# A two-part vision kernel on one core: the next image's moments moved, the picks in fewer instructions, and motif rows left out at the edges

## What is computed

```python
# feature: (2, 128, 128, 96); G = 16 groups of Cg = 8 planes, K = 3
slices = [feature[:, :, ki:ki + Hm, kj:kj + Wm] for ki in range(K) for kj in range(K)]  # Hm = 126, Wm = 94
motif = stack(slices).reshape(B, G, 9, Cg, L)
gram = einsum('bgjcl,bgjdl->bgjcd', motif, motif)
d2 = sq[..., :, None] + sq[..., None, :] - 2.0 * gram        # the diagonal set to inf
nn_idx = argmin(d2, axis=-1)
u_max = max(nn_idx, axis=-1)
c_max = sum(nn_idx == u_max[..., None], axis=-1)
motif_nn = take_along_axis(motif, u_max[..., None, None], axis=3)
term = floor(motif * motif_nn * c_max[..., None, None] / Cg)
ser2 = (motif * batch_mask + term).reshape(B, G, Cg, 9, Hm, Wm)
for k in range(9):                                            # ki, kj = k // 3, k % 3
    out[:, :, :, ki:ki + Hm, kj:kj + Wm] += ser2[:, :, :, k]
x = x + out
```

## Time and profile before

| | us |
|---|---|
| median of 3 runs | 1446.81 (1444.57 to 1449.93) |
| the profiled execution | 1437.17 |
| its span | 1435.4 |
| TensorE busy | 1302.0 (91%) |
| VectorE busy | 1123.1 (78%) |
| ScalarE busy | 887.5 (62%) |
| GpSimd busy | 635.8 (44%) |

### The profile page before, as it was taken

One profiled execution on the slowest core, in us unless ns is written; L12 is line 12 of the kernel. 1 busy time (PEld: TensorE's weight loads), 2 busy tenths in 40 slices (PEclk: granted clock), 3 DMA queues, 4 the chain that ended last, 5 costly groups with the idle time before them and its releaser, 6 DMA issues. The chain is left out here.

```text
span 1435.4 us, 34146 instructions
## 1 busy us (share of the span) xinstructions
PE 1302.0 (91%) x13586; PEld 1051.4 (73%) x13586; DVE 1123.1 (78%) x1896; ACT 887.5 (62%) x1013; POOL 635.8 (44%) x672
## 2 busy tenths in 40 slices
PE   3899999986999499999979999999779959999998
PEld 1799997985999255555549999989679945555554
DVE  6587775568763799999967777737877739999998
ACT  3567663212552499999956666531145419999996
POOL 4889992442220253343039999624323114444400
PEclk9999999998999699999999999999989969999999
DMA  5466731892134345464427886239105234264433
GB/s 218 129 210 214 218 96 32 255 262 118 46 132 180 132 138 126 127 166 101 133 86 225 255 250 189 75 107 275 35 2 243 112 136 142 78 179 119 139 74 106
DMA packets 77173, 210.28 MB, mean 146 GB/s; under 512 B 15450, under 2 KB 15558, under 8 KB 74326
## 3 DMA queue, kind: packets, MB, share of 16 engines
q1 hardware_dynamic: 62510, 158.10, 35.0%
q0 software_dynamic: 6720, 36.93, 9.7%
q10 hardware_dynamic: 7784, 13.07, 3.3%
HBM read 91.54 MB, written 67.04 MB: 110 GB/s over the span
## 5 line engine op out<-in xcount | busy, mean ns | idle before, releaser
L1780 PE MATMUL acc<-rnd,ident 128*128 128x376 f32 x1152 | 392.8, 484 | 13.6 <-ACT rnd L1757 13.6
L1780 PEld LDWEIGHTS acc<-rnd,ident 128*128 128x128 f32 x1152 | 216.8, 192 | 134.5 <-ACT rnd L1757 15.0
L954 PE MATMUL ps_a<-wa,shared 128*128 128x192 f16 x1536 | 295.0, 246 | 2.6 <-DMA xc<-low 1.5
L954 PE MATMUL ps_a<-wb,xb 128*128 128x192 f16 x1536 | 294.0, 245 | 0.0
L1752 ACT ACTIVATE rnd_m<-prod,plus_round,scale 128x1504 f32<-128x1504 f32 x144 | 235.6, 1636 | 38.8 <-DVE prod L1603 29.5
L1716 DVE SCALAR_TENSOR_TENSOR over<-prod,scale,rnd 128x1504 bf16<-128x1504 f32 x144 | 255.0, 1773 | 0.0
L572 POOL TENSOR_TENSOR vt<-z 96x256 f32<-96x256 f32 x248 | 241.6, 995 | 3.8 <-ACT z L848 3.6
L1757 ACT ACTIVATE rnd<-rnd_m,minus_round 128x1504 f32<-128x1504 f32 x144 | 223.2, 1550 | 4.7
L1660 POOL DMA_INDIRECT near<-f_planes,index x42 | 120.4, 2867 | 148.0 <-DVE prod L1603 141.9
L954 PE MATMUL ps_a<-wfa,shared 128*128 128x96 f16 x1536 | 155.7, 206 | 5.9 <-issue 5.6
L954 PE MATMUL ps_a<-wfb,xb 128*128 128x96 f16 x1536 | 155.8, 205 | 0.9 <-issue 0.9
(11 more groups left out here) (344 smaller groups left out, 2463.9 us busy)
## 6 DMA issues: line engine op xcount, KB each, us to landing
xb<-shared ACTq DMA_DIRECT2D x64, 195.0 KB, 2.8
f_planes<-img SPq DMA_DIRECT2D x8, 1536.0 KB, 14.2
shared<-f_planes SPq DMA_DIRECT2D x16, 768.0 KB, 5.5
v_a<-shared SPq DMA_DIRECT2D x40, 260.0 KB, 2.6
v_b<-xb SPq DMA_DIRECT2D x40, 260.0 KB, 3.0
shared<-v_a SPq DMA_DIRECT2D x40, 260.0 KB, 4.4
xb<-v_b SPq DMA_DIRECT2D x40, 260.0 KB, 5.1
v_c<-xc SPq DMA_DIRECT2D x40, 195.0 KB, 3.5
```

The costliest lines, as they stand in the source:

```text
L954: mm = lambda a, w, first, end: nc.tensor.matmul(out(i), a, w, start=first, stop=end)
L1780: nc.tensor.matmul(o(m), k["ident"][:, :], rnd[:, n % RNDS, BR * m:BR * m + BR, :], start=False, stop=False, skip_group_check=True)
```

## The change

There are three edits.

1. The moments of image 1 are computed in `motif_grams` of image 0 instead of in `motif_terms`. Their small tiles lie in `x_next`, whose contents are used up by then, and their sums in the PSUM bank `ps_s`.
2. The picks leave out a copy of the PSUM tile `nnt` (it is read from PSUM twice instead), and two of the small operations are merged into others. Two results that the next instruction does not read are no longer waited for.
3. A step of `motif_terms` works on the rows that `valid(n)` names: at slab 0 one row less for ki = 1 and two less for ki = 2, at slab 7 two less for ki = 0 and one less for ki = 1. The memsets of the edge rows and the semaphore `edged` go.

```diff
@@ ScalarE in motif_grams, ahead of its copies into g_half
+            if x_after is not None:
+                group_stats_root(nc, act, k, next_sums, next_mom, att_sems["stat_summed"], att_sems["stat_rooted"])
             for j in (0, 2):
                 act.wait_ge(chunk_done, C // CHUNK + j // 2)
@@ TensorE in motif_grams, behind last_column()
+            def next_summed(step, line):
+                pe.wait_ge(att_sems["stat_ready"], step + 1)
+                nc.tensor.matmul(next_sums[:, step, :], k["mean_ones"][:, :], next_part[:, line, :], start=True,
+                                 stop=True).then_inc(att_sems["stat_summed"], 1)
+
+            def next_columns():
+                pe.wait_ge(att_sems["mom_row"], 1)
+                for j in range(2):
+                    last = nc.tensor.matmul(next_col[0:C, j:j + 1], next_mom_c[0:1, j, :], k["ident"][0:1, 0:1],
+                                            start=True, stop=True)
+                last.then_inc(att_sems["mom_col"], 1)
+
             for side in range(2):
                 for m_ in range(m, BLOCKS):
+                    if x_after is not None and side == 0 and m_ == m:
+                        next_summed(0, 3)
                     gram(m_, range(8 * side, 8 * side + 8))
+                if x_after is not None:
+                    if side == 0:
+                        next_summed(1, 1)
+                    else:
+                        next_columns()
@@ VectorE in motif_grams, ahead of its copies into g_half
+            if x_after is not None:
+                channel_moments(nc, dve, c, k, next_part, next_mom, next_mom_c, next_sums, next_col, att_sems)
             for j in (1, 3):
                 dve.wait_ge(chunk_done, C // CHUNK + j // 2)
@@ the picks, VectorE
-            c.then_wait(nc.vector.tensor_copy(nnt, ps_a[1][0:MG, 0:MR]))
+            nnt = ps_a[1][0:MG, 0:MR]
-            c.then_wait(nc.vector.tensor_tensor(t1, u, jj_less, ALU.subtract))
-            c.then_wait(nc.vector.tensor_scalar(ge, t1, 0.0, None, ALU.is_ge))
-            c.then_wait(nc.vector.tensor_scalar(t1, t1, float(KK), None, ALU.add))
+            nc.vector.scalar_tensor_tensor(t1, u, float(KK), jj_less, ALU.add, ALU.subtract)
+            c.then_wait(nc.vector.tensor_tensor(ge, u, jj_less, ALU.is_ge))
             c.then_wait(nc.vector.scalar_tensor_tensor(ku, ge, -float(KK), t1, ALU.mult, ALU.add))
-            c.then_wait(nc.vector.scalar_tensor_tensor(cu, ge, -1.0, jj, ALU.add, ALU.add))
-            c.then_wait(nc.vector.tensor_scalar(t1, ku, 3.0, None, ALU.is_ge))
-            c.then_wait(nc.vector.tensor_scalar(t2, ku, 6.0, None, ALU.is_ge))
-            c.then_wait(nc.vector.tensor_tensor(kui, t1, t2, ALU.add))
+            nc.vector.scalar_tensor_tensor(cu, ge, -1.0, jj, ALU.add, ALU.add)
+            c.then_wait(nc.vector.tensor_scalar(t2, ku, 3.0, None, ALU.is_ge))
+            c.then_wait(nc.vector.scalar_tensor_tensor(kui, ku, 6.0, t2, ALU.is_ge, ALU.add))
@@ motif_terms
+        def valid(n):
+            i, sh = steps[n]
+            dy = TAPS[sh][0]
+            return max(dy - R * i, 0), min(R, HM + dy - R * i)
...
-            fv = fc[:, s, :].rearrange("p (r c) -> p r c", c=C)[:, :, dx:dx + WM]
+            lo, hi = valid(n)
+            fv = fc[:, s, :].rearrange("p (r c) -> p r c", c=C)[:, lo:hi, dx:dx + WM]
...
-            nc.gpsimd.memset(near[:, 0, 0:2 * C], 0.0).then_inc(edged, 1)
...
-            if b + 1 < B:
-                channel_moments(nc, dve, c, k, part, mom, mom_c, next_sums, next_col, att_sems)
...
-                nc.vector.scalar_tensor_tensor(over[:, n % 2], prod[:, n % PRODS], scale[:, sh:sh + 1],
-                                               rnd[:, n % RNDS], ALU.mult, ALU.is_lt).then_inc(over_done, 1)
+                rows = slice(*valid(n))
+                nc.vector.scalar_tensor_tensor(over[:, n % 2, rows], prod[:, n % PRODS, rows], scale[:, sh:sh + 1],
+                                               rnd[:, n % RNDS, rows], ALU.mult, ALU.is_lt).then_inc(over_done, 1)
```

More of the change, by code:

```diff
@@ L1123, in motif_grams @@
         mn = sb("mn", [MR, MG], F32)
-        nnt, eq2 = (g_half[0:MG, j, 0:MR] for j in range(2))
+        eq2 = g_half[0:MG, 1, 0:MR]
         sel = g_half[0:MG, 2, 0:6 * KK].rearrange("p (v j) -> p v j", j=KK)
@@ L1140, in motif_grams @@
         sums = lambda: ps_s[:, 0:2 * GN].rearrange("p (a g) -> p a g", g=GN)
+        if x_after is not None:
+            x_flat = x_next[:].rearrange("p a c -> p (a c)")
+            next_part = x_flat[:, 0:4 * GN].rearrange("p (a g) -> p a g", g=GN)
+            next_mom = x_flat[:, 4 * GN:6 * GN].rearrange("p (a g) -> p a g", g=GN)
+            next_mom_c = x_flat[0:1, 6 * GN:6 * GN + 2 * C].rearrange("p (a c) -> p a c", c=C)
+            next_sums, next_col = sums(), ps_s[:, 2 * GN:2 * GN + 2]
         piece = lambda j: img[:, :, PIECE * j:PIECE * j + PIECE]
@@ L1559, in motif_terms @@
         acc = [ctx.enter_context(nc.psum_tensor(f"acc{s}_{b}", [P, R // BR, 512], F32)) for s in range(2)]
[L1560 to L1563, removed]
+        (own, scaled, indexed, prod_v, prod_p, rm_done, rnd_done, over_done, acc_done, out_ready, last_rows) = (
+            sem(n) for n in ("t_dve", "scaled", "indexed", "prod_v", "prod_p", "rm_done",
                              "rnd_done", "over_done", "acc_done", "out_ready", "last_rows"))
@@ L1751, in _ @@
                     act.wait_ge(rnd_done, n - 1)
-                nc.scalar.activation(rnd_m[:, n % 2], prod[:, n % PRODS], ACT.Identity,
+                rows = slice(*valid(n))
+                nc.scalar.activation(rnd_m[:, n % 2, rows], prod[:, n % PRODS, rows], ACT.Identity,
                                      bias=k["plus_round"][:, 0:1], scale=scale[:, sh:sh + 1]).then_inc(rm_done, 1)
@@ L1756, in _ @@
                     act.wait_ge(acc_done, n - RNDS + 1)
-                nc.scalar.activation(rnd[:, n % RNDS], rnd_m[:, n % 2], ACT.Identity,
+                nc.scalar.activation(rnd[:, n % RNDS, rows], rnd_m[:, n % 2, rows], ACT.Identity,
                                      bias=k["minus_round"][:, 0:1]).then_inc(rnd_done, 1)
@@ L1767, in _ @@
                 if sh == 0:
-                    if i == 0 and b + 1 < B:
-                        channel_moments_sums(nc, pe, k, part, mom_c, next_sums, next_col, att_sems)
-                    if i == 1 and b + 1 < B:
-                        pe.wait_ge(att_sems["mom_col"], 2)
                     if i >= 2:
@@ L1776, in _ @@
                                          start=True, stop=False, skip_group_check=True)
-                o = lambda m: bank[:, m, 0:BR * C].rearrange("p (r c) -> p r c", c=C)[:, :, dx:dx + WM]
+                lo, hi = valid(n)
+                spans = [(m, max(lo - BR * m, 0), min(hi - BR * m, BR)) for m in range(R // BR)]
+                o = lambda m, a, e: bank[:, m, 0:BR * C].rearrange("p (r c) -> p r c", c=C)[:, a:e, dx:dx + WM]
                 pe.wait_ge(rnd_done, n + 1)
-                for m in range(R // BR):
-                    nc.tensor.matmul(o(m), k["ident"][:, :], rnd[:, n % RNDS, BR * m:BR * m + BR, :], start=False,
+                for m, a, e in spans:
+                    nc.tensor.matmul(o(m, a, e), k["ident"][:, :], rnd[:, n % RNDS, BR * m + a:BR * m + e, :], start=False,
                                      stop=False, skip_group_check=True)
                 pe.wait_ge(over_done, n + 1)
-                for m in range(R // BR):
-                    last = nc.tensor.matmul(o(m), k["minus_ident"][:, :], over[:, n % 2, BR * m:BR * m + BR, :],
+                for m, a, e in spans:
+                    last = nc.tensor.matmul(o(m, a, e), k["minus_ident"][:, :], over[:, n % 2, BR * m + a:BR * m + e, :],
                                             start=False, stop=(sh == KK - 1), skip_group_check=True)
```

13 lines of the change are left out of this document (2 added, 11 removed).

## The result

The changed kernel took 1433.79 us (median of 13 runs, 1428.63 to 1440.93) against 1444.89 us for the kernel before (13 runs, 1435.75 to 1450.81) in the same comparison: 0.9936 of its time, interval 0.9915 to 0.9957, some 9 us less. The first three of the latter 13 runs are those behind the median of 1446.81. The forecast of 1441.4 us was too high and the range of 1437.0 to 1445.5 missed the median.

The account below looks back on a forecast made before the run. VectorE was taken to pace the terms at 3.33 us a step, and a chain between engines to bound the end of `motif_grams`. -6.4 - 1.7 - 0 + 2.7 = -5.4 us from 1446.81 gave 1441.4, range 1437.0 to 1445.5.

Parts of the forecast that it names:

- Rows: Terms, slabs 0 and 7: shorter VectorE steps save 3.5 us an image, 0.3 lost waiting at product 58; 6.4 us less.
- third rival: Terms: moves of neighbour rows cost slab 7 its whole gain, rows worth 3.5 us, sum -2.5, 1444.3 us; chance 0.08.
- Picks: Chain before the terms, VectorE alone at work: fewer operations and waits save 0.85 us an image, 1.7 us in all.
- The moments' old place: Start of image 0's terms: the moments lay wholly under the gathers, so removing them is worth 0 (bounds 0 and 0.1).
- first rival: Start of image 0's terms: moments were on the path, gaining 3.24 us; sum -8.6, 1438.2 us; chance 0.10.
- Their new place: End of image 0's Gram chain: sums 0.5 and 0.4, turn and copy 1.85; 2.7 us more (bounds 1.6 and 3.5).
- second rival: Gram chain: the moments' sums prolong TensorE's low clock, costing 2 us; sum -3.4, 1443.4 us; chance 0.17.
- thin stretch: TensorE's small matmuls in `last_column`, 446.83 to 451.72 us, behind which its clock was said to fall to 1.2 GHz.
- The sum: Whole kernel: -6.4 - 1.7 - 0 + 2.7 = -5.4 us, carried from 1446.81 to 1441.4 us.
- faster by over 0.5%: Whole kernel: chance 0.21 of a gain above 0.5% (7.2 us); 0.75 for within 0.5%, 0.04 for slower.

Follow-up runs that it names:

- e5: The changed kernel run again, unaltered, against the kernel before: 1438.41 us, ratio 0.999.
- e1: Only the rows left out in `motif_terms`, moments and picks as in the kernel before: 1435.48 us, ratio 0.9946 to the kernel before.
- e10: Rows left out and picks shortened, moments in their old place, against the kernel before: 1436.52 us, ratio 0.9953.
- e12: Kernel before plus six more zero matmuls per image ahead of the attention's mixing matmuls: 1440.79 us, ratio 1.0 to the kernel before.

## Why the prediction was off, step by step

- **Rows.** Forecast 6.4 us less. The price of a row held (0.10 each for product and `over`), and nine rows at 0.196 make 1.76 us for each of the two slabs. Over the eleven profiles with the edit on VectorE and the six without any part of it, product 2 to 24 (slab 0) became 1.70 and 1.65 us shorter in images 0 and 1, and product 54 to 70 (slab 7) 1.38 and 1.35, where 1.76 - 0.3 stood. The wait of product 58 alone grew by 0.55 in image 0 and 0.58 in image 1, nearly all of the 0.6 saved ahead of it. Over products 58, 59 and 63 together the waits grew by 0.39 in either image. That is the 0.6 less 0.2 of the prediction's own pieces, where it took 0.3. The four savings together are 6.1 us of the 6.4. The middle, which no edit touches, came out 0.5 and 0.2 us longer, no clear difference beside its scatter (0.2 to 0.6 from profile to profile), so the whole terms became 2.6 and 2.8 us shorter, 5.4 together. The third rival (3.5) falls.
- **Picks.** 1.7 forecast, 0.87 an image measured, 1.74. By the Trainium skill (VectorE: DVE Perf Modes, on the TRN2 errata) reads from PSUM would have given some of it back; L1529 reads PSUM in 0.22 us, as L1499 read SBUF, so here they didn't.
- **The moments' old place.** 0 forecast, 0 measured: in image 0 product 2 stood 13.96 to 14.67 us behind the start with them there and 14.09 to 14.43 without; in image 1, 13.81 to 14.37. The first rival falls.
- **Their new place.** 2.7 forecast, 2.1 to 2.2 measured, in four profiles, two with each length of the low clock. The way from the turn of the moments to that of `g_half` was 1.61 us in e5, where 1.85 stood, which leaves some 0.5 for the two sums, where 0.9 stood.
- **The clock in the Gram chain.** The second rival happened in the first profile, but e1, e10 and e12 (whose code there is that of before) show it without the moved moments, and e5 doesn't show it with them. The edit doesn't cause it, and where the low clock is longer it costs 1.2 us, not 2. What the prediction calls a thin stretch was not an idle one: TensorE was busy for 5.00 of 5.00 us, with small matmuls. The Trainium skill (TensorE: Matmul & The Clock Gate, Part 1) has it that throttled is the default state and activity releases it; the clock did come back in each of these profiles, and that the edit would put off its release is not borne out.
- **The sum.** By the marks: 5.4 + 1.74 + 0 - 2.1 = 5.0 us less; by the 37 runs, 5.7, give or take 1.6. Forecast 5.4. That the sum comes so near is in part luck: the rows gave 1.0 less than forecast and the moments cost 0.6 less.
- **The step that failed** is "That execution was 9.6 us below the median of its runs, so I carry the difference over: 1446.81 - 5.4 = 1441.4". The median of three runs was taken for the kernel's own. Over 158 runs the same kernel's median is 1442.2, 4.6 less; medians of three drawn from those runs lie between 1438.3 and 1446.8 in 8 of 10 draws. From 1442.2 the same sum gives 1436.8, and the changed kernel's 37 runs have the median 1437.2. The rest of the miss, 3.4 us, is luck of the first comparison, as far as is known: its 13 runs lay below those of the two later ones, and its interval (0.9915 to 0.9957) just leaves out the 0.996 of all runs. No edit and no stage is shown to be behind that.
- The range failed by the same step: it allowed for the costs of the edits and too little for the scatter of both medians, which is the larger part here. And "faster by over 0.5%" with 0.21 was too sure of its opposite: at 0.4% of true gain, comparisons of a dozen runs gave 0.64, 0.10 and 0.37%.

## What to carry to other kernels

Read the median shown as a draw. Here three runs gave 1446.81 and the profiled execution 1437.17, and the kernel's own time, 1442.2, lay in between; the range must hold the draw as well as the edit. An edit of a few microseconds is judged by marks in the trace, differences of starts around its place, and by marks of untouched stages as the control. Work hidden under a transfer (the moments under the gathers) is free where it stands; moved into a chain it costs, so by the marks the change is better without edit 1, by 2.1 us, though the runs are too few to show it.

## What was not expected of the hardware

- The granted clock of one program differs from execution to execution in its unchanged parts. Low stretches at the end of the Gram products last 3.4 or 6.8 us in the profiles of one and the same program, and the mixing matmuls of the attention run at 2.4 GHz in most profiles and at 1.2 GHz for 13.7 us in three, at a cost of some 5 us each. Over all runs a run's time goes with its mean clock (0.947 to 0.968) by about 7.4 us per 0.01. In the runs of the kernel before over half of the variance (a correlation of -0.75 over 145 runs) goes with the clock; what makes the clock differ is not shown.
- Small instructions on VectorE that are not waited for follow each other 0.09 us apart (479.08 and 479.17 in the changed kernel's picks), against 0.19 with the wait.
- Six further matmuls of zeros an image, in gaps of 0.4 us, on an engine that is busy 91% of the span, went with 4 us less (give or take 2.6) than the parts give apart, in the presence of two edits elsewhere. The time was the lowest in all three comparisons; the cause is not explained.
